# Four convolution layers on one core: the first layer's scratch rows laid out row by row, and 25 instead of 27 rounds of matmuls in its first block

## The chip, the cores and the metric

One core of a Trainium2 chip runs the whole program. The metric is the device time of one execution in microseconds (us), lower is better. Engines are named as the profile names them: PE is TensorE (PEld its weight loads), DVE is VectorE, ACT is ScalarE, POOL is GpSimd, SP is SyncE, which issues most of the DMAs. A name with a q behind it (SPq, ACTq) is an engine's queue as it issues DMAs.

## What is computed

The input x is (4, 16, 512, 512), float32. Four layers follow, each of the form x = x + conv(gn(x)), where gn is a group norm over pairs of channels. Only the first layer's two blocks are touched by the change:

```
def _conv_reflect(x, w, bias, dil, pad):
    xp = jnp.pad(x, ((0, 0), (0, 0), (pad, pad), (pad, pad)), mode='reflect')
    out = lax.conv_general_dilated(xp, w, window_strides=(1, 1), padding='VALID', rhs_dilation=(dil, dil), ...)
    return out + bias[None, :, None, None]

def _denoise_block(x, w1, b1, w2, b2, w3, b3, a, b, c):
    trip = _triplets(x)          # each channel with the one before and after it: (B*T, 3, H, W)
    o = a*_conv_reflect(xf, w1, b1, 1, 2) + b*_conv_reflect(xf, w2, b2, 2, 4) + c*_conv_reflect(xf, w3, b3, 4, 8)
    return jnp.tanh(o).reshape(B, T, H, W)

y = _denoise_block(gn(x), blk1 ...)
z = _denoise_block(y, blk2 ...)
x = x + z
```

So each block is a 5x5 convolution at dilations 1, 2 and 4 over three neighbouring channels, summed and put through tanh. The later layers are a 3x3 convolution on quantized values, a box filter of 17x17, and a complex convolution between two Fourier transforms.

## The kernel before

**Values as two halves.** A float32 value goes to TensorE as a high and a low float16. A row in the DRAM scratches `xs` (input of block 1) and `ys` (output of block 1, input of block 2) is `RW` = 1056 float16: the high row of 528 (512 and 8 mirrored columns at either side), then the low row of 528; 2112 bytes.

**Chunks, groups, units.** An image has 8 pairs of channels. A unit u is one half (256 rows) of one pair of output channels; block 1 is u = 0 to 63, block 2 is u = 64 to 127. A unit has four groups g, a group four chunks of 16 rows; the running number of a group is n = 4u + g. A chunk's window holds 32 rows (16 and 8 above and below) of four channels: 128 partitions. The windows of a unit's 16 chunks are the tile `c_w` (`win[half]`, 128 x 16 x 1056); two of them alternate. For p > 0 only the 64 partitions of the new channel pair are loaded, since the other pair is there from two units before.

**Products (line 734).** A matmul takes a weight matrix of 128 x 32 (32 = 16 rows x 2 channels) and 512 columns of one chunk's window, shifted by one of nine column offsets. Four of them, for the four chunks of a group, fill the 128 partitions of a PSUM bank: one round. There are nine column offsets and three products of halves for each (high x high, high x low, low x high): 27 rounds in block 1. Block 2 uses that offsets -2, -1, 1, 2 need only the middle 24 rows, so 96 partitions: its weight and row order puts those 24 rows into partitions 0 to 95, and copies bring low rows into the free 32. `near` (`c_n`, copied by VectorE, lines 669 and 670) holds the 96 partitions of high rows with 32 of low rows below them; `twice` (`c_2`, copied by ScalarE, lines 817 and 818) holds the remaining 64 low partitions once for each of two offsets. Eight rounds become four on `near` and two on `twice`: 25. The copies of group n + 1 are made at the start of the loop's turn for group n, on both engines.

**What follows a group.** ScalarE evicts with tanh (`evict`, line 812). In block 1 VectorE makes the high half (`halves`, line 639) and the low half (line 641) in `c_y`, POOL mirrors the pads (line 911), and SP stores two to three copies of each channel's rows to `ys` (`store_y`, line 974); in units where SP's queue is crowded POOL issues those stores (line 882). In block 2 VectorE adds x, and takes statistics and extremes (lines 649 to 658), and SP stores x1.

**The input's way into block 1.** The normalized input is made beside the products, one tile of 8 x 16 rows x 16 for a channel pair at a time (32 tiles): four steps, one in each of four groups that follow one another, a tile every seven groups. v0 takes statistics on VectorE (lines 465, 467), v1 (line 473) and v2 (lines 477 to 481) the spread, the root and the scaling, v3 the low half (line 487). In the group after v0 and after v1 TensorE sums over the partitions with two small fp32 matmuls, 15 rounds into the group (lines 711, 715). ScalarE makes the root and the high half (line 803). POOL mirrors pads (line 859), SP stores to `xs` (line 929). Group 15 also holds VectorE's `channel_weights` (lines 556 to 585) for later layers, group 22 `scaled_weights`, and from u = 60 on a table.

**Order on SP.** In each group SP loads the window part of unit u + 2 that TensorE has just left (line 956 in block 1: four chunks a group, two DMAs for each channel pair; line 952 in block 2: eight chunks every second group, four DMAs), then stores. Before the loop it loads units 0 and 1. In DRAM the scratches of the kernel before keep, for a channel pair, [row in chunk 16][channel 2][chunk 32][RW], so that the chunks of one partition follow one another: 4 x 2112 bytes are one piece in block 1, 8 x 2112 in block 2.

## Time and profile before

| | |
|---|---|
| median of three runs | 5166.97 us (5162.87 to 5169.14) |
| the profiled execution | 5166.33 us |
| its span | 5164.4 us |
| PE busy | 4871.3 us (94%) |
| DVE busy | 3723.3 us (72%) |
| ACT busy | 3384.5 us (66%) |
| POOL busy | 1510.5 us (29%) |
| mean granted clock of TensorE | 0.989 |
| DMA | 1167.24 MB, 226 GB/s |

How to read it: "busy" is the share of the span in which an engine had an instruction; matmuls are pipelined, so PE at 94% is not PE at its peak. A timeline row gives start, duration, engine and line, what it writes and reads, how many alike follow one another, and in brackets the idle time before it with what ended it. DMA share is the mean busy share of the 16 DMA engines, and may pass 1 where packets of one engine overlap. PEclk is the granted clock of TensorE, 1.00 for the 2.4 GHz level and 0.50 for the 1.2 GHz level.

### The profile page before, as it was taken

The page shows a single profiled execution, that of the slowest core. Times are in us where ns is not written, and L with a number is a line of the kernel's source. Part 1 is how long each engine was busy: PE and PEld are TensorE (multiplying, and loading weights), DVE is VectorE, ACT ScalarE, POOL GpSimd, SP SyncE. Part 2 cuts the span into 40 slices and gives each one's busy share as a digit, 9 for nine tenths or more (in the row PEclk, how much of TensorE's full clock was granted, in tenths as well). Part 3 has the DMA queues.
Part 4 walks back from the last instruction along what each step waited for, and adds up shares of the span by engine and source line. Part 5 has one row for each costly group of instructions (what it writes and reads, how often), then busy time and mean ns, then how long its engine had stood idle before and what let it go on. Part 6 is the DMA issues. An engine that isn't in the chain of part 4 may idle for free. (4 is left out here: it accounts for less than half of the span.)

```text
span 5164.4 us, 176760 instructions
## 1 busy us (share of the span) xinstructions
PE 4871.3 (94%) x76605; PEld 2923.4 (57%) x76605; DVE 3723.3 (72%) x6707; ACT 3384.5 (66%) x3511; POOL 1510.5 (29%) x1801
## 2 busy tenths in 40 slices
PE   4999999999999999999999979997777899999998
PEld 2444544444447967568875533444555566666665
DVE  4653553553534888888888868887999688888888
ACT  1222222231224888888888878885998798989897
POOL 1102102102102221222222100003776355555556
PEclk9999999999999999999999989999999999999999
DMA  8778778778757877878787769996886466666664
GB/s 259 232 247 267 234 247 267 238 246 258 236 191 204 242 222 229 237 223 238 233 226 241 223 221 325 323 324 238 308 309 261 111 151 152 150 154 149 154 149 119
DMA packets 368016, 1167.24 MB, mean 226 GB/s; under 512 B 75689, under 2 KB 76328, under 8 KB 297386
## 3 DMA queue, kind: packets, MB, share of 16 engines
q1 hardware_dynamic: 342040, 1131.78, 72.2%
q0 software_dynamic: 23040, 21.76, 1.5%
q8 instruction: 606, 9.93, 0.8%
q10 hardware_dynamic: 2162, 2.39, 0.2%
q14 instruction: 168, 1.38, 0.1%
HBM read 683.58 MB, written 453.51 MB: 220 GB/s over the span
## 5 line engine op out<-in xcount | busy, mean ns | idle before, releaser
L734 PE MATMUL c_p<-c_w,wc 128*32 128x512 f16 x27648 | 1518.7, 380 | 25.3 <-DMA c_w<-xs 19.9
L812 ACT ACTIVATE c_t<-c_p,cbias,cscale 128x512 f32<-128x512 f32 x512 | 397.9, 777 | 1273.7 <-PE c_p L734 1273.7
L734 PEld LDWEIGHTS c_p<-c_w,wc 128*32 128x32 f16 x27648 | 753.1, 96 | 762.3 <-issue 26.6
L734 PE MATMUL c_p<-c_w,w 128*32 128x512 f16 x19456 | 1145.0, 379 | 3.5 <-issue 3.4
L734 PEld LDWEIGHTS c_p<-c_w,w 128*32 128x32 f16 x19456 | 758.5, 96 | 316.3 <-issue 7.1
L639 DVE TENSOR_SCALAR c_y<-c_t 128x512 f16<-128x512 f32 x256 | 111.8, 437 | 644.7 <-ACT c_t L812 593.6
L1818 PE MATMUL f_P<-f_qh,f_wt 64*64 64x512 f16 x4608 | 545.7, 378 | 1.8 <-DVE f_t L1714 1.8
L1818 PE MATMUL f_P<-f_hl,f_wt 64*64 64x512 f16 x4608 | 545.3, 379 | 0.0
L817 ACT ACTIVATE c<-c_w 64x2052 f16<-64x2052 f16 x256 | 492.5, 1924 | 11.9 <-DMA c_w<-ys 5.7
L818 ACT ACTIVATE c<-c_w 64x2052 f16<-64x2052 f16 x256 | 492.9, 1925 | 6.2
L1979 POOL TENSOR_TENSOR f_y<-f_y,f_x 128x512 f32<-128x512 f32 x256 | 330.8, 1292 | 449.2 <-DVE f_hl L1693 443.1
L1578 POOL TENSOR_TENSOR e_hl<-e_g,e_hl 128x2048 f16<-128x2048 f32 x63 | 257.2, 4082 | 610.4 <-ACT e_hl L1528 610.4
L1714 DVE SCALAR_TENSOR_TENSOR f_t<-f_P,f_kk,f_ci 128x256 f32<-128x256 f32 x1024 | 423.5, 476 | 13.0 <-PE f_P L1818 7.9
L911 POOL COPY c_y<-c_y 128x16 f16<-128x16 f16 x512 | 87.6, 202 | 1129.6 <-DVE c_y L641 1129.6
L1779 PE MATMUL f_qp<-f_hil,f_gT 128*128 128x260 f16 (+1 forms) x3120 | 392.2, 275 | 4.0 <-DVE f_qh L1698 4.0
L1818 PEld LDWEIGHTS f_P<-f_hl,f_wt 64*64 64x64 f16 x4608 | 233.0, 106 | 255.0 <-issue 77.7
L1207 PE MATMUL d_pp<-d_q,wq 128*128 128x512 f16 x1536 | 346.4, 381 | 17.7 <-DVE d_q L1104 17.7
L1985 POOL TENSOR_TENSOR f_t<-f_t 128x512 f32<-128x512 f32 (+1 forms) x260 | 333.1, 1281 | 70.6 <-DVE f_hl L1693 70.6
L1953 ACT ACTIVATE f_y<-f_P,f_kk,sv 128x256 f32<-128x256 f32 x512 | 260.8, 560 | 128.1 <-PE f_P L1818 121.9
L649 DVE TENSOR_TENSOR a_x<-c_t,a_x 128x512 f32<-128x512 f32 x256 | 190.8, 745 | 193.6 <-ACT c_t L812 178.8
L1779 PEld LDWEIGHTS f_qp<-f_hil,f_gT 128*128 128x128 f16 (+1 forms) x3120 | 294.6, 98 | 41.8 <-issue 5.0
L734 PE MATMUL c_p<-c_n,w 128*32 128x512 f16 x4096 | 314.3, 379 | 0.0
(275 smaller groups left out, 7826.3 us busy)
## 6 DMA issues: line engine op xcount, KB each, us to landing
c_w<-xs SPq DMA_DIRECT2D x576, 264.0 KB, 8.2
d_x<-x SPq DMA_DIRECT2D x128, 1024.0 KB, 7.6
x<-d_x SPq DMA_DIRECT2D x128, 1024.0 KB, 5.1
c_w<-ys SPq DMA_DIRECT2D x144, 528.0 KB
xs<-a_hl SPq DMA_DIRECT2D x70, 1056.0 KB, 11.1
a_x<-in_x SPq DMA_DIRECT2D x256, 256.0 KB, 5.7
a_x<-in_x SPq DMA_DIRECT2D x128, 512.0 KB, 4.8
x<-a_x SPq DMA_DIRECT2D x512, 128.0 KB, 6.1
```

The source lines that it names most:

```text
L734: t = p.matmul(pg[32 * j:32 * j + 32, :], weights[:, var], source[:, j, at:at + NW], start=start, stop=stop, tile_position=(0, 32 * j))
L812: s.activation(tt_[n % 3][:, :], pp[:, n % 4, :], ACT.Tanh, bias=cbias[:, blk:blk + 1], scale=cscale[:, blk:blk + 1]).then_inc(c_act, 1)
L817: s.activation(twice[n % 2][64:128, :, PAD - 2:PAD - 1 + NW], w[0:64, :, PW + PAD + 1:PW + PAD + 2 + NW], ACT.Copy).then_inc(c_2b, 1)
L818: s.activation(twice[n % 2][0:64, :, PAD - 2:PAD - 1 + NW], w[0:64, :, PW + PAD - 2:PW + PAD - 1 + NW], ACT.Copy).then_inc(c_2a, 1)
L1207: t = p.matmul(pp[:, 4 * (i % 2) + j, :], wq[:, wl, dx, :], qt[i % NQ][:, j, dx:dx + NW], start=(i < 2 and dx == 0 and wl == 0), stop=(i > ...
L1578: q.tensor_tensor(h[:, 1], gt[i % 2][:, :, :], h[:, 0], ALU.subtract).then_inc(e_lo, 1)
L1714: v.scalar_tensor_tensor(dst[0:n, z], src[:, 256 * z:256 * z + 256], k_[0:n, off + z:off + z + 1], cc_[0:n, j, z], op, ALU.mult).then_inc( ...
L1779: t = p.matmul(qp[0:n, a_, 0:260], T[:, xl, 1 - a_, kx, 0:n], hil[:, wl, 1 - a_, kx, :], start=z == 0, stop=z == 5)
L1818: t = p.matmul(P[64 * z:64 * z + 64, bank, :].rearrange("p (a i) -> p a i", a=2), w[k0:k0 + 64, wl, f, :], r[k0:k0 + 64, l, :, 0:256], sta ...
L1953: s.activation(y0[i % 3][0:n, z], P[0:n, 0, 256 * z:256 * z + 256], ACT.Identity, bias=k_[0:n, 6 + z:7 + z], scale=inv(i)).then_inc(f_y0, 1)
L1979: q.tensor_tensor(y0[i % 3][:, :, :], y0[i % 3][:, :, :], par(xin[i % NXF][:, :]), ALU.add).then_inc(f_ax, 1)
L1985: q.tensor_tensor(t1[i % 3][0:n], t1[i % 3][0:n], t2[i % 2][0:n], ALU.add).then_inc(f_aw, 1)
```

## The change

In the first layer:

- `xs` and `ys` are laid out row by row: [row 512][channel 2][RW] for a pair of channels. `constants()` orders the selection matrix by the new places of rows.
- A store of y names 64 rows as one dimension instead of 4 x 16. A store of the input names rows of 2112 bytes instead of pieces of four.
- Both blocks load windows as block 2 did in time and size (eight chunks, after every second group), now as one part of 48 (row, channel) places and two of 8 for each channel pair, of 2112 bytes each; at an image's upper and lower end the parts leave out the rows that aren't there, and one more part of 40 is loaded.
- Both blocks make `near` and `twice` and run 25 rounds. In block 1 VectorE makes three of the copies and ScalarE one; in block 2 two and two, as before.
- In block 1 the high half of y moves from VectorE to ScalarE (`high`), with its wait for earlier stores.
- The weights of both blocks stand in one tile in the same row order (`wall`), so the 24 reordering DMAs of u = 8 to 19 and their semaphore go, POOL makes the near weights once at the start, for both blocks, and clears two chunks' windows at the image's ends, and the swapped copy of the weights is made with two DMAs of the whole tile.

The diff, cut:

```diff
-        self.xs = nc.dram_tensor("xs", (NB, NC // 2 + 1, 16, 2, 32, RW), F16).ap()
-        self.ys = nc.dram_tensor("ys", (NB, NC // 2 + 1, 16, 2, 32, RW), F16).ap()
+        self.xs = nc.dram_tensor("xs", (NB, NC // 2 + 1, NH, 2, RW), F16).ap()
+        self.ys = nc.dram_tensor("ys", (NB, NC // 2 + 1, NH, 2, RW), F16).ap()
...
             e.wait_ge(c_ld[u % 2][g // 2], 16 * (3 + at_edge(u % 2, g)) * n)
...
-                def halves(u, g):
+                def low(u, g):
...
-                    v.wait_ge(c_act, n + 1)
-                    if u >= 2 and g == 0:
-                        stored(v, u)
-                    elif g == 0:
-                        v.wait_ge(a_sd, n_xs(2))
-                    v.tensor_scalar(hi, tl[:, :], YS, None, ALU.mult).then_inc(c_hi, 1)
                     v.wait_ge(c_hi, n + 1)
                     v.scalar_tensor_tensor(lo, tl[:, :], YS, hi, ALU.mult, ALU.subtract).then_inc(c_lo, 1)
...
                     v.tensor_copy(near[n % 2][0:96], w[0:96, :, 0:PW]).then_inc(c_nh, 1)
                     v.tensor_copy(near[n % 2][96:128], w[64:96, :, PW:RW]).then_inc(c_nl, 1)
+                    if n < 4 * NU:
+                        v.tensor_copy(twice[n % 2][0:64], w[0:64, :, PW:RW]).then_inc(c_2a, 1)
...
                     for di in (2, 3, 5, 6):
-                        t = four(wu[:, 1, :, di], rows4, PAD + DX[di])
-                    if not blk:
-                        for di in (2, 3, 5, 6):
-                            for xl in range(2):
-                                t = four(wu[:, 0, :, di], rows4, xl * PW + PAD + DX[di], stop=(di, xl) == (6, 1))
-                    if blk:
...
+                        four(wu[:, blk, 1, :, di], rows4, PAD + DX[di])
+                    if n == 0:
+                        p.wait_ge(w_wn, 12)
+                    wnear = wn[pr % 2][:, blk]
+                    p.wait_ge(c_nh, n + 1)
+                    p.wait_ge(c_nl, n + 1)
+                    for e, di in enumerate((2, 3, 5, 6)):
+                        four(wnear[:, :, e], near[n % 2], PAD + DX[di])
+                    p.wait_ge(*((c_2c, n - 4 * NU + 1) if blk else (c_2a, n + 1)))
+                    p.wait_ge(c_2b, n + 1)
+                    four(wnear[:, :, 4], twice[n % 2], PAD - 2)
+                    t = four(wnear[:, :, 5], twice[n % 2], PAD - 1, stop=True)
...
+                def high(u, g):
+                    n = 4 * u + g
+                    s.wait_ge(c_act, n + 1)
+                    if u >= 2 and g == 0:
+                        stored(s, u)
+                    elif g == 0:
+                        s.wait_ge(a_sd, n_xs(2))
+                    s.activation(yt[u % 2][:, g, 0, PAD:PAD + NW], tt_[n % 3][:, :], ACT.Copy, scale=YS).then_inc(c_hi, 1)
...
-                        q.dma_start(dram(ys, pair(b, gp, slot, 16 * half) + g * 4 * RW, [[RW, 4], [VP, 16], [1, RW]]), y[m::2]).then_inc(c_yp[u % 2], 16)
+                        q.dma_start(dram(ys, pair(b, gp, 256 * half + 64 * g, slot), [[YP, 64], [1, RW]]), y[m::2]).then_inc(c_yp[u % 2], 16)
...
-                        e.dma_start(dram(xs, pair(b, gp, slot), [[VP, 16], [4 * RW, 8], [1, 4 * RW]]),
-                                    halves_of(i)[c][:, :, :, :].rearrange("p r l w -> p (r l w)")).then_inc(a_sd, 16)
+                        e.dma_start(dram(xs, pair(b, gp, 0, slot), [[YP, 16], [64 * YP, 8], [16 * YP, 4], [1, RW]]),
+                                    halves_of(i)[c][:, :, :, :].rearrange("p r l w -> p r (l w)")).then_inc(a_sd, 16)
...
+                    f, n = int(first), 8 - first - last
+                    parts = [(0, 48, -4, f, n), (96, 8, -8, f, 8 - f), (112, 8, 20, 0, 8 - last)]
+                    parts += [(16, 40, 0, 0, 1)] * first + [(0, 40, -4, 7, 1)] * last
                     for gp in (0, 1) if p == 0 else (p + 1,):
...
+                        for to, count, row, j, banks in parts:
+                            e.dma_start(win[half][to + gp % 2:to + 2 * count:2, 4 * g + j:4 * g + j + banks],
+                                        dram(src, pair(b, gp, 256 * half + 64 * g + 16 * j + row), [[RW, count], [16 * YP, banks], [1, RW]])).then_inc(c_ld[half][g // 2], 16)
...
-                        if u + 2 < NU and not late:
-                            load(u + 2, g)
-                        if NU <= u + 2 < 2 * NU and g % 2:
+                        if u + 2 < 2 * NU and not late and g % 2:
                             load(u + 2, g - 1)
```

## Rows read from the trace of the kernel before

**Rows 1.** The page's engine line, and line 734 by tiles: count, ns min/median/max, first and last start.
```profile
PE 4871.3 (94%) x76605; PEld 2923.4 (57%) x76605; DVE 3723.3 (72%) x6707; ACT 3384.5 (66%) x3511; POOL 1510.5 (29%) x1801
...
L734 PE MATMUL c_p<-c_w,wc x27648: 377/379/634, 70.9 to 1631.3; 128*32 128x512 f16 x199
...
L734 PE MATMUL c_p<-c,w x2048: 377/379/391, 1636.4 to 3023.4; 128*32 128x512 f16 x187
```

**Rows 2.** Timeline of ACT in block 1: start us, duration us, line, operands [idle before].
```profile
805.15 0.78 ACT L812 ACTIVATE c_t<-c_p,cbias,cscale 128x512 f32<-128x512 f32 x1 [6.17 <-PE c_p L734]
811.42 0.78 ACT L812 ACTIVATE c_t<-c_p,cbias,cscale 128x512 f32<-128x512 f32 x1 [5.49 <-PE c_p L734]
...
819.24 3.62 ACT L803 ACTIVATE a_hl<-a_x 128x4096 f16<-128x4096 f32 x1 [0.78 <-DVE a_x L481]
...
829.35 0.78 ACT L812 ACTIVATE c_t<-c_p,cbias,cscale 128x512 f32<-128x512 f32 x1 [5.06 <-PE c_p L734]
835.19 0.78 ACT L812 ACTIVATE c_t<-c_p,cbias,cscale 128x512 f32<-128x512 f32 x1 [5.06 <-PE c_p L734]
```

**Rows 3.** Timeline of ACT in block 2.
```profile
1902.24 0.78 ACT L812 ACTIVATE c_t<-c_p,cbias,cscale 128x512 f32<-128x512 f32 x1 [0.73 <-PE c_p L734]
1903.04 1.92 ACT L817 ACTIVATE c<-c_w 64x2052 f16<-64x2052 f16 x1
...
1907.64 0.78 ACT L812 ACTIVATE c_t<-c_p,cbias,cscale 128x512 f32<-128x512 f32 x1 [0.73 <-PE c_p L734]
```

**Rows 4.** Timeline of PE: the longest waits in block 1.
```profile
128.63 5.34 PE L734 MATMUL c_p<-c_w,wc 128*32 128x512 f16 x60 [7.63 <-DMA c_w<-xs]
...
198.54 0.59 PE L794 MATMUL a_p<-c2b,ones 128*128 128x1 f32 x2 [4.78 <-DVE c2b L585]
...
502.28 3.18 PE L734 MATMUL c_p<-c_w,wc 128*32 128x512 f16 x28 [3.64 <-DMA c_w<-xs]
...
1273.20 10.63 PE L734 MATMUL c_p<-c_w,wc 128*32 128x512 f16 x168 [5.26 <-DMA c_w<-xs]
```

**Rows 5.** Busy time by stretch: engines, PEclk, DMA share, GB/s; after such a wait.
```profile
502.00:506.00 4.00, 3.72 (x36) 1.40 (x40) 3.78 (x7) 0.00 (x0) 2.65 (x6) 0.50 1.01 344
```

**Rows 6.** Timeline of DVE in block 2: the copies into near.
```profile
1905.56 0.70 DVE L669 COPY c_n<-c_w 96x2112 f16<-96x2112 f16 x1
1906.29 0.70 DVE L670 COPY c_n<-c_w 32x2112 f16<-32x2112 f16 x1
```

**Rows 7.** Timeline of DVE in block 1, over the steps of one input tile.
```profile
800.09 4.84 DVE L465 BATCH_NORM_STATS2 a_st<-a_x 128x6 f32<-128x512 f32 x8
804.96 0.37 DVE L467 BATCH_NORM_AGGREGATE a_mv<-a_st 128x2 f32<-128x48 f32 x1
806.03 0.43 DVE L639 TENSOR_SCALAR c_y<-c_t 128x512 f16<-128x512 f32 x1 [0.70 <-ACT c_t L812]
806.49 0.69 DVE L641 SCALAR_TENSOR_TENSOR c_y<-c_t,c_y 128x512 f16<-128x512 f32 x1
...
822.89 4.47 DVE L487 TENSOR_TENSOR a_hl<-a_x,a_hl 128x4096 f16<-128x4096 f32 x1 [2.50 <-ACT a_hl L803]
```

**Rows 8.** Timeline of DVE: the start of the channel weights; first and last of the scaled ones.
```profile
179.16 0.60 DVE L556 COPY rp<-a_p 128x432 f32<-128x432 f32 x1
...
230.82 0.15 DVE L245 TENSOR_SCALAR c2b<-a_p 128x1 f32<-128x1 f32 x1
...
240.57 0.15 DVE L541 TENSOR_SCALAR sv<-sv 128x1 f32<-128x1 f32 x1
```

**Rows 9.** Busy time by stretch, columns as in rows 5: three short stretches by their DMAs.
```profile
1542.00:1545.00 3.00, 3.00 (x64) 1.63 (x56) 0.15 (x1) 0.78 (x1) 0.17 (x1) 1.00 0.24 86
1871.00:1873.00 2.00, 2.00 (x44) 1.19 (x39) 1.97 (x4) 1.98 (x2) 0.00 (x0) 1.00 1.19 270
883.00:886.00 3.00, 3.00 (x64) 1.49 (x60) 0.80 (x2) 0.00 (x0) 2.70 (x6) 1.00 1.04 304
```

**Rows 10.** DMA queue over 1542 to 1545 us: packets, MB, share of 16 engines.
```profile
q1 hardware_dynamic: 129, 0.26, 23.6%
```

More of the change, by code:

```diff
@@ L17 @@
 RW = 2 * PW
-CP = 32 * RW
-VP = 2 * CP
+YP = 2 * RW
 DX = [-8, -4, -2, -1, 0, 1, 2, 4, 8]
@@ L40, in slot @@
     def slot(row, chan):
-        h8, s = ((1, 0), (0, 0), (1, 1), (0, 1))[row // 8 + 1]
-        v8 = row + 8 * h8 - 16 * s
-        return 8 * (2 * v8 + chan % 2) + 4 * s + 2 * h8 + chan // 2
+        place = row + (32, 4, 4, 4, 4, 4, 4, 8)[row // 4 + 2]
+        return 4 * place + 2 * (chan % 2) + chan // 2
     sel = np.zeros((27, 3, 32, 128), np.float32)
@@ L397, in stored, with at_edge @@
                     e.wait_ge(done[u % 2], n)
-        def n_win(u, g):
-            return sum((1 + (place(r)[2] == 0)) * (64 * (g % 2 == 0) if place(r)[0] else 32) for r in range(u % 2, u + 1, 2))
+        def at_edge(half, g):
+            return (half, g // 2) in ((0, 0), (1, 1))
         def rows_in(e, u, g):
-            if place(u)[0]:
-                g = g // 2 * 2
-            e.wait_ge(c_ld[u % 2][g], n_win(u, g))
-        def doubled(n):
-            return 4 * NU <= n < 8 * NU
-        def n_copied(n):
-            return n - 4 * NU + 1
+            n = sum(1 + (place(r)[2] == 0) for r in range(u % 2, u + 1, 2))
+            e.wait_ge(c_ld[u % 2][g // 2], 16 * (3 + at_edge(u % 2, g)) * n)
         def four_rows(e, n):
@@ L420, in four_rows @@
             rows_in(e, u, g)
[L421 removed]
+            if n >= 2:
+                e.wait_ge(c_pe, n - 1)
             return win[u % 2][:, 4 * g:4 * g + 4]
[L424 to L429 removed]
         def table_of(u):
@@ L684, in _ @@
                 v0(2), v1(2)
+                copies(0)
                 for u in range(2 * NU):
@@ L700, in _ @@
                             table(table_of(u), g // 2)
-                        (total if blk else halves)(u, g)
+                        (total if blk else low)(u, g)
                         if blk:
@@ L838, in _ @@
                 s.wait_ge(a_v, mark["wc"])
+                copies(0)
                 for u in range(2 * NU):
@@ L848, in _ @@
                         evict(u, g)
+                        if u < NU:
+                            high(u, g)
                         if st_ == 2:
```

95 lines of the change are left out of this document (33 added, 62 removed).

## The prediction

> **What bounds the kernel now.** I read the page first, then single lines: TensorE is busy 94% of the span, and the matmuls of the first layer alone run from 70.9 us to 3023.4 us of 5164.4, block 1 until 1631.3 and block 2 after it [rows 1]. Nothing outside these two blocks is changed, so the question is what ends one group of four chunks in each. The ACT timeline gives the period, since one eviction (line 812) closes each group: 835.19 - 829.35 = 5.84 us in block 1 [rows 2], 1907.64 - 1902.24 = 5.40 us in block 2 [rows 3]. Block 1 has 27 rounds of four matmuls in a group and block 2 has 25; 5.84 / 27 and 5.40 / 25 are both 0.216 us. So both blocks run at the pace of TensorE. Two groups of each input tile last 6.26 us (811.42 - 805.15 = 6.27 [rows 2]): the two small fp32 matmuls of the statistics cost 0.42 us each. Beside that there are single stalls on loaded windows and on VectorE's chain for the later layers [rows 4], and a stall of some length is paid twice: from 502 to 506 us the granted clock is 0.50 [rows 5], the 1.2 GHz level, after the wait of 3.64 us.
>
> **The sum is made against 5166.3 us**, the profiled execution's own time (span 5164.4 and 1.9 around it); the median of the runs is 5167.0, so the two stand for each other.
>
> **Two rounds fewer in block 1.** 27 rounds become 25 in 256 groups: 0.216 x 2 = 0.432 us each. The first eight groups give nothing: group 8 waits 7.63 us for its window [rows 4] at 128.6, a chain of tile 2 (split, mirrored pads, store, load) through SP that starts no earlier than now, so a faster TensorE only waits longer. I count 248 x 0.432 = -107 us. The window of group 8 now comes in one piece of eight chunks instead of four, which I put at +1.5 us (bounds -3 and +4, about one load more).
>
> **Copies that both blocks now need.** In block 2 this work is there already: VectorE's two copies 0.70 us each [rows 6], ScalarE's 1.92 us each [rows 3]. Block 1 adds to VectorE three copies and takes away the high half (0.43 us [rows 7]): with the spacing of 0.73 from start to start, +2.2 - 0.46. ScalarE gets one copy of 1.92 and the high half: 4096 elements cost 3.62 us [rows 2], so 512 cost about 0.45 plus a fixed part of some 0.2, an estimate of 0.64. Mean load of VectorE: 2.2 + 0.6 + (5.24 + 0.8 + 4.4 + 4.4) / 7 = 4.9 of 5.4 us; ScalarE: 1.9 + 0.8 + 0.6 + (3.6 + 2.8) / 7 = 4.2. Neither is the bound on average, but the order within a group matters, for VectorE takes its work in program order.
> Group k ends at 0. Eviction 0.78, high half 0.64, low half 0.61 and the hand-overs: low(k) is done at 2.2. Copies for the next group but one 2.2: 4.4. If a tile's first step lies here, eight statistics and their sum take 5.24 (800.09 to 805.33 [rows 7]): 9.7. TensorE wants that result 15 rounds into the group after: 5.40 + 15 x 0.216 = 8.65. It waits **1.0 us**, where before it did not (2.0 + 5.2 = 7.2 against 5.84 + 3.24 = 9.1). The following steps fit: after the low half of the input (4.4 us, line 487 [rows 7]) the near copies come 1.7 us before their group asks for them. 28 tiles: +28 us, bounds 0 (if copies run beside statistics better than I add them) and 50 (a wait of 1.8, with POOL's pads in the way of the copies). A wait of 1 us is short of the 3.64 that cost clock.
> **VectorE's long chains.** The channel weights hold VectorE from 179.16 until TensorE gets c2b at 198.54 [rows 8, 4], 19.4 us. Before, TensorE waited 4.78 us for them, and lost some 3.4 us more to the slower clock (as after 502 us: 28 matmuls in 3.18 us where 1.5 are due [rows 4]). Now the copies of group 17 are queued behind that chain: low(14) ends 5.5 us after its group (a tile's last step lies before it), copies 2.2, chain 19.4, low half and first copies 2.1, together 29.2; group 17 asks at 2 x 5.4 + 19 x 0.216 + 0.9 = 15.8. Wait 13.4, with clock 16.8, against 8.2: +8.7. The scaled weights (230.82 to 240.72 [rows 8]) cost nothing before; now the copies of group 24 lie behind them, wait about 5.6 and 3.4 of clock: +9.
>
> **Stores over 64 rows.** Each store of y names 64 rows of 2112 bytes; before, its DRAM side has an outer dimension of 4. From 1542 to 1545 us, with these stores alone in flight, the DMA share is 0.24, so 3.8 of 16 engines work, and a packet takes 0.236 x 48 / 129 = 0.09 us [rows 9, 10]. In one u (four groups) these four engines carry 144 of them, 13.4 us; loads 18 packets of 8448 bytes at 4 x 0.110 (304 GB/s over 16 engines, 883 to 886 us [rows 9]) 7.9; the input's stores 4.0 and the input's loads 3.5 at the same price: 28.8 us against the 24.4 that a u took. So these prices are a fifth too high, and those four engines were full; this is why windows came late at the image boundary (3.64 and 5.26 us [rows 4], with clock 6.6 each).
> The Trainium skill (DMA: Bandwidth & Descriptors, Why a DMA increments its semaphore by 16 and not by 1) says that the engines used are the largest number up to 16 that divides the outermost dimension of both sides; by that rule, the trace agrees: 4 gives 3.8.
> After: 36 packets on every engine, 3.3 us.
> **Input tiles of 48, 8 and 8 rows, packets of 2112 bytes.** A window half takes 64 x 8 packets: three on each engine for each of eight chunks from the 48 rows, and if the 8 rows go to eight engines, 16 more there. At 0.110 and, for the 8 rows, at the price of block 2's loads (1871 to 1873 us: 270 GB/s at a share of 1.19, 0.148 us for 2112 bytes of a packet's own time [rows 9]) that is 2.6 + 2.4 = 5.0 us, 11.3 in a u (2.25 halves). Input store 4.0, input load 3.5, y 3.3: 22.1 us on the fullest engines; divided by the same 1.18, 18.7, against TensorE's 4 x 5.40 + 0.9 = 22.5. So DMA stays under TensorE, with some 17% to spare, and costs nothing while that holds. The two boundary stalls and a smaller third (about 16 us) mostly go: -12. In block 2 the fullest engines go from 5 x 1.19 to 5.0 us for a half: -3, or nothing.
> The Trainium skill (SBUF — State Buffer, Door 1: The DMA port swizzle) speaks against this tile shape: sixteen neighbouring partitions reach only 4 of 16 ports, about 109 GB/s, so that each 8-row part (135 KB) would take an estimated 1.24 us however many engines work on it. The sum by it would be 155 instead of 148 ns for these packets, 0.3 us in a u. No row shows the parts alone.
> **Small things.** The row-major layout keeps the bytes. SP issues 7 loads in a u instead of 9. The wait for y's stores goes from VectorE to ScalarE; it was rare. Weights for both blocks are now made once at the start by POOL (twelve short copies), hidden behind the statistics; the swap of partitions waits for them, ahead of u = 2, which alone needs it.
> **Sum:** 5166.3 - 107 + 1.5 + 28 + 8.7 + 9 - 12 - 3 = **5092 us** (5091.5).
>
> **Rivals.**
> (a) TensorE never waits in block 1: copies and statistics overlap enough. 5092 - 28 = 5064 us. For: block 2's VectorE does 5 us of work in 5.4 without a stall. Against: the order above.
> (b) The DMA engines become the bound of block 1. If the fullest need 23.1 to 23.9 us in a u, block 1 lasts 64 x 23.1 = 1478 to 1530, plus 19 for the start, against 1560: 5103 to 5155, and most likely about 5125. For: 22.1 at full price is close to 22.5, and the bytes of block 1 pass in 1450 us instead of 1560. Against: the same prices overstate today's load by a fifth.
> (c) Slower than before, the same place with a price that decides: all load packets at the dearest rate and more. It decides from 24.1 us in a u (64 x 24.1 + 19 = 1561), and that is what comes out if all 90 load packets, not the 36 of the 8-row parts alone, cost 0.148: 13.3 + 10.8. With 10% more for each, a cost of short packets that no row shows, it is 25.4, block 1 lasts 1645 and the whole 5251 us.
> (d) The change doesn't do what it says: y's stores stay on few engines. 13.4 + 11.3 + 7.5 = 32 us in a u, 27 with the factor, +170 us. Against: the outer dimension is 64 on both sides.
>
> **How the numbers follow.** Forecast 0.55 (own range 5072 to 5112), (a) 0.13, (b) 0.24, (c) and (d) 0.08. The range leaves out the top of (b), (c), (d) and the bottom of (a): 5056 to 5150. Less than 0.2% (10 us), which a measurement of this kernel can't tell from no change, is 5157 to 5177: the ends of (b) and (c) that meet there. Faster 0.85, same 0.08, slower 0.07.
>
> **What would show it.** Eviction spacing in block 1 of 5.40; matmuls on c_n and c from the start; PE waiting about 1.0 us for line 467's result once a tile; waits of 13 and 6 us near groups 17 and 24; no DMA share of 0.24 with y's stores in flight; no wait for a window near 500 and 1270 us. Wrong if TensorE waits for windows in steady state (b, c), or if near copies come late in each tile (VectorE over its bound).

## The result, and the profile after

The changed kernel takes 5135.65 us (median of five, 5130.48 to 5147.41) against 5166.97 us before: a ratio of 0.9947, 95% interval 0.9929 to 0.9964. The sign of the forecast held; of the forecast gain of 75 us less than half came (31.3). The time lies outside the forecast's own range (5072 to 5112 us) and inside its wider one (5056 to 5150), where the prediction had placed rival (b). The page's engine line after (busy us, share of the span, instructions), and its line of the DMA queue that SP feeds (packets, MB, share of 16 engines), beside [rows 1]:

```profile
PE 4773.7 (93%) x74557; PEld 2754.2 (54%) x74557; DVE 4136.3 (81%) x7219; ACT 4039.4 (79%) x4023; POOL 1627.4 (32%) x1803
q1 hardware_dynamic: 486200, 1126.77, 75.7%
```

TensorE is busy for 97.6 us less than before, more than the time fell by: it waits more. What it waits for in block 1, by the view of waits from 80 to 1610 us (engine, tile, line; released by; us in total, times, longest):

```profile
PE c_p L710 <- DMA c_w<-xs: 52.1, 10, 13.0
PE a_p L690 <- DVE a_mv L449: 24.3, 26, 3.5
PE c_p L710 <- DVE c_n L646: 18.4, 2, 13.0
PE c_p L710 <- issue: 5.1, 11, 0.9
```

The second and the third line are waits that the prediction named, in its sizes. The first is not: 52.1 us for windows, of which the prediction had left group 8's (7.63 and 1.5) and the first window's, 3.4 before and 13.0 now. Where they lie, from PE's timeline (start, duration, operands, count [idle before, releaser]), beside [rows 4]:

```profile
80.49 5.93 PE L710 MATMUL c_p<-c_w,wc 128*32 128x512 f16 x76 [13.03 <-DMA c_w<-xs]
...
147.33 5.76 PE L710 MATMUL c_p<-c_w,wc 128*32 128x512 f16 x60 [11.91 <-DMA c_w<-xs]
220.36 1.90 PE L710 MATMUL c_p<-c_n,wc 128*32 128x512 f16 x16 [12.97 <-DVE c_n L646]
266.89 1.90 PE L710 MATMUL c_p<-c_n,wc 128*32 128x512 f16 x16 [5.43 <-DVE c_n L646]
504.22 4.29 PE L710 MATMUL c_p<-c_w,wc 128*32 128x512 f16 x76 [1.16 <-DMA c_w<-xs]
520.96 5.85 PE L710 MATMUL c_p<-c_w,wc 128*32 128x512 f16 x76 [5.19 <-DMA c_w<-xs]
```

The first two are the first window and group 8's; the last two are the second image's start, the kind of place where windows were late before too. The waits of 13.03, 12.97, 11.91, 5.43 and 5.19 us are followed by slow matmuls (76 of them in 5.93 or 5.85 us instead of 4.29, 16 in 1.90 instead of 1.04); the one of 1.16 is not.

**Where the time went, by stretches.** One eviction closes a group, so the times between evictions in ACT's timeline divide both blocks without gaps. "Start" is everything until group 8's eviction (n = 8); "boundaries" are n = 57 to 68, 122 to 136 and 186 to 200, around the three changes of image; "clear" is the rest of block 1 from n = 26 on. The column "forecast" takes the prediction's terms to the same stretches (with 0.432 us for each group, the first ones too; so its sum is 3 us more than the prediction's).

| stretch | before | after | difference | forecast |
|---|---|---|---|---|
| start, to n = 8 | 137.1 | 155.7 | +18.6 | -1.9 |
| n = 8 to 16 | 50.9 | 46.7 | -4.2 | -3.4 |
| n = 16 to 26, VectorE's long chains | 67.6 | 79.5 | +11.9 | +13.4 |
| clear, 190 groups | 1133.3 | 1073.2 | -60.1 | -54.1 |
| three boundaries, 39 groups | 242.8 | 249.2 | +6.4 | -28.9 |
| block 2 (n = 255 to 511) | 1392.1 | 1385.5 | -6.6 | -3 |
| last eviction | 3023.8 | 2989.9 | -33.9 | -77.9 |

The miss of 44 us stands in two rows: 20.5 at the start, 35.3 at the boundaries, and 12 given back by the others. Both are places where TensorE waits for windows. So the question for the runs was what makes a window late there, and whether the parts that came as forecast came for the forecast reason.

### The profile page after: what moved, and what is told of

Same layout as the page of the kernel before. It is cut to its first block and busy times, and to the rows that moved or that the text cites. A ratio compares the mean times of both kernels' runs of the same rounds, so it can differ in the third digit from the quotient of the medians.

```text
span 5128.7 us, 174422 instructions
## 1 busy us (share of the span) xinstructions
PE 4773.7 (93%) x74557; PEld 2754.2 (54%) x74557; DVE 4136.3 (81%) x7219; ACT 4039.4 (79%) x4023; POOL 1627.4 (32%) x1803
## 5 line engine op out<-in xcount | busy, mean ns | idle before, releaser
L710 PE MATMUL c_p<-c_w,wc 128*32 128x512 f16 x38912 | 2271.3, 380 | 56.7 <-DMA c_w<-xs 52.1
L710 PEld LDWEIGHTS c_p<-c_w,wc 128*32 128x32 f16 x38912 | 1202.4, 96 | 979.0 <-DMA c_w<-xs 44.3
L800 ACT ACTIVATE c<-c_w 64x2052 f16<-64x2052 f16 x512 | 984.7, 1923 | 95.9 <-DMA c_w<-xs 83.7
L710 PE MATMUL c_p<-c_n,wc 128*32 128x512 f16 x8192 | 587.7, 380 | 19.1 <-DVE c_n L646 18.4
L899 POOL COPY c_y<-c_y 128x16 f16<-128x16 f16 x512 | 191.1, 401 | 973.2 <-DVE c_y L617 973.2
L802 ACT ACTIVATE c<-c_w 64x2052 f16<-64x2052 f16 x256 | 492.9, 1925 | 6.3
L645 DVE COPY c_n<-c_w 96x2112 f16<-96x2112 f16 x512 | 389.2, 760 | 61.3 <-DMA c_w<-xs 61.3
L1693 DVE SCALAR_TENSOR_TENSOR f_t<-f_P,f_kk,f_ci 128x256 f32<-128x256 f32 x1024 | 423.6, 476 | 12.7 <-PE f_P L1797 7.4
L617 DVE SCALAR_TENSOR_TENSOR c_y<-c_t,c_y 128x512 f16<-128x512 f32 x256 | 177.2, 692 | 269.3 <-ACT c_y L796 267.3
L710 PEld LDWEIGHTS c_p<-c_n,wc 128*32 128x32 f16 x8192 | 268.6, 96 | 217.5 <-DVE c_n L645 19.3
L646 DVE COPY c_n<-c_w 32x2112 f16<-32x2112 f16 x512 | 368.3, 719 | 15.9
L710 PE MATMUL c_p<-c,wc 128*32 128x512 f16 x4096 | 365.1, 380 | 0.9 <-issue 0.9
```

Of the source, the lines that this page charges most:

```text
L645: v.tensor_copy(near[n % 2][0:96], w[0:96, :, 0:PW]).then_inc(c_nh, 1)
L646: v.tensor_copy(near[n % 2][96:128], w[64:96, :, PW:RW]).then_inc(c_nl, 1)
L710: t = p.matmul(pg[32 * j:32 * j + 32, :], weights[:, var], source[:, j, at:at + NW], start=start, stop=stop, tile_position=(0, 32 * j))
L800: s.activation(twice[n % 2][64:128, :, PAD - 2:PAD - 1 + NW], w[0:64, :, PW + PAD + 1:PW + PAD + 2 + NW], ACT.Copy).then_inc(c_2b, 1)
L802: s.activation(twice[n % 2][0:64, :, PAD - 2:PAD - 1 + NW], w[0:64, :, PW + PAD - 2:PW + PAD - 1 + NW], ACT.Copy).then_inc(c_2c, 1)
L1693: v.scalar_tensor_tensor(dst[0:n, z], src[:, 256 * z:256 * z + 256], k_[0:n, off + z:off + z + 1], cc_[0:n, j, z], op, ALU.mult).then_inc( ...
```

## The experiments

The times below are medians, the ratios are to the kernel before on the same chip, whose median there was 5162.0 us (runs 1 to 4), 5174.9 (5 to 7), 5166.7 (8 to 10) and 5165.8 (11 and 12). Differences between runs of different groups carry these few us with them. Where a rate of the loads is given, it is that of a stretch near 75 us, before the loop, in which only window loads are in flight.

**1. The two parts of 8 rows as one of 16.** The rows in places 48 to 63 are not the right ones; bytes and packets are kept but for 8 places more in the chunk at an image's end.

```diff
-parts = [(0, 48, -4, f, n), (96, 8, -8, f, 8 - f), (112, 8, 20, 0, 8 - last)]
+parts = [(0, 48, -4, f, n), (96, 16, 0, 0, 8)]
```

> Edit: the two 8-row parts of each window load become one part of 16 (row, channel) places, the same bytes and the same number of 2112 byte packets, so the outer rows of every window hold other rows than they should (this part of the computation is changed). Theory A, the parts of 8 places are what makes the loads slow, since they keep to eight engines: the loads alone (66 to 80 us, 207 GB/s in the changed kernel, 281 before) come back to about 280 GB/s, the first matmul of line 710 starts at 76 instead of 80.5, the waits for windows of block 1 (52 us) fall under 20, and the time is about 5105 us. Theory B, packets of 2112 bytes instead of 8448 are slow by themselves: 207 GB/s stays, and the time stays at 5136 within 5. Theory C, sixteen neighbouring partitions are too few: the rate rises only a little, to 230 GB/s, 5125 us.

Measured: 5140.5 us, ratio 0.9951 (0.9935 to 0.9966), as the change itself. But not the same inside: start 145.8 (-9.9), boundaries 227.4 (-21.8), and the clear stretch 1098.6 (+25.4). The waits from 80 to 1610 us:

```profile
PE c_p L710 <- issue: 37.8, 38, 1.9
PE c_p L710 <- DVE c_n L646: 18.6, 2, 13.1
PE a_p L690 <- DVE a_mv L449: 17.5, 20, 1.9
PE c_p L710 <- DMA c_w<-xs: 12.3, 1, 12.3
```

The late windows at the boundaries are gone, though the rate rose hardly (219 GB/s from 74 to 80 us, 206 in the changed kernel). I read this as the work of how evenly the 16 engines are loaded, though no row shows the engines singly. In their place came waits for "issue", that is, for nothing that the profile names. A look at one, PE's timeline:

```profile
643.89 2.11 PE L710 MATMUL c_p<-c_w,wc 128*32 128x512 f16 x36
647.76 1.48 PE L710 MATMUL c_p<-c_w,wc 128*32 128x512 f16 x24 [1.76 <-issue]
```

The DMA records of the instruction queue (q8) have a packet of 16 KB that lands at 646.14 us, 1.6 before the matmuls go on; the ones that land at 637.24 and 654.83 stand 1.5 and 1.7 before the ends of two more such waits. Of the 45 gaps of over 1.2 us from one matmul's start to the next between 300 and 2950 us, 29 have an instruction packet that lands 1.2 to 1.8 us before their end (44 of 56 in run 12 below). Of all moments 8 to 9% have one, and of the 28 such gaps in the changed kernel 3, so no more than chance. I read this as TensorE's own program arriving late behind the data. No run takes the fetches away, so it stays a reading.

**2. The kernel before with its load as four pieces of a row.** Meant to show what shorter packets cost by themselves.

```diff
-    win[half][gp % 2 + 2 * h8:128:4, 4 * g:4 * g + 4].rearrange("p k w -> p (k w)"), ... [[CP, 16], [RW, 2], [1, 4 * RW]]
+    win[half][gp % 2 + 2 * h8:128:4, 4 * g:4 * g + 4], ... [[CP, 16], [RW, 2], [RW, 4], [1, RW]]
```

> Edit: the kernel before, only block 1's window loads walk four pieces of 2112 bytes instead of one of 8448; partitions, engines, order and bytes are the same. Theory B (short packets are slow by themselves): the loads alone from 66 to 80 us fall from 281 to about 210 GB/s, windows come late at the start and at the image boundaries, 5190 us or more. Theory A: 270 to 280 GB/s stay, 5167 us within 8.

Measured: 5163.67 us, ratio 1.0004 (0.9991 to 1.0017). The packets in the trace stayed at 8448 bytes: pieces that follow one another on both sides are one piece, however they are written. The run says nothing on short packets; it shows how far the stretches of one kernel differ between two profiles (boundaries 235.9 and 242.8, start 138.4 and 137.1).

**3. The change with 27 rounds and without copies in block 1**, so layout, loads and the moved high half alone.

```diff
+if not blk:
+    for di in (2, 3, 5, 6):
+        for xl in range(2):
+            t = four(wu[:, 0, 0, :, di], rows4, xl * PW + PAD + DX[di], stop=(di, xl) == (6, 1))
+    t.then_inc(c_pe, 1)
+    return
```

> Edit: the changed kernel, but block 1 runs its 27 rounds straight from the windows and makes no copies; layout, loads, stores and the move of the high half stay. If DMA bounds the start and the image boundaries and TensorE the rest, evictions stand 5.84 us apart in steady state, the first matmul starts late as in the changed kernel (80 us against 70.9), and the boundaries wait less than in the changed kernel, since TensorE asks later; sum: 5167 + 9 + about 10 for group 8, less some boundary time, 5175 us (5165 to 5190). Rival: the loads cost nothing and VectorE's copies made the whole shortfall: 5160 or less, as the stores' better spread would then show alone.

Measured: 5176.54 us, ratio 1.0028 (1.0012 to 1.0043): the layout alone costs some 14 us. The start is the changed kernel's (154.9 us), so the loss there has nothing to do with the copies. The boundaries take 234.6 us, 5.2 over what 39 groups need without any wait (229.4, 5.88 us a group with the small matmuls of two tiles); with 25 rounds they take 249.2, 36.7 over it (212.5). Fewer rounds made the boundaries no shorter but longer: TensorE comes earlier to a window that comes no earlier (it waits 23.8 us for windows there, and 2.4 in this run).

**4. The first step of a tile ahead of the copies in VectorE's order.**

```diff
+if s == 0:
+    v0(i)
 if 4 * u + g + 1 < 8 * NU:
     copies(4 * u + g + 1)
-if i is not None:
+if i is not None and s:
```

> Edit: the changed kernel, but VectorE takes a tile's statistics (v0) ahead of the copies of the next group, in the same turn of the loop. My step says that TensorE's wait of 0.9 us for them in each of 27 tiles (24.3 us in all) is on the path: it goes, and the time is 5136 - 24 = 5112 us. Rival: in block 1 the DMAs are the bound on average, so what is won here is given back as longer waits for windows: 5130 or more, with the waits for c_w risen from 52 us.

Measured: 5116.77 us, ratio 0.9906 (0.9882 to 0.9929), 19 us less than the change. TensorE's waits for the statistics between 80 and 1610 us fell from 24.3 us (26 times) to 2.3 (once). The copies are early enough even after 5 us of statistics, so the tile term came from the order of the two. The waits for issue rose from 5.1 to 14.2 us, so not all that was won shows in the time.

**5. Windows as one part of 64 places.** The rows stand in another order than the weights expect. Bytes and packets are kept but for the chunk at an image's end, of which 64 places are loaded instead of 48; the DMAs of a channel pair fall from three to one.

```diff
-parts = [(0, 48, -4, f, n), (96, 8, -8, f, 8 - f), (112, 8, 20, 0, 8 - last)]
-parts += [(16, 40, 0, 0, 1)] * first + [(0, 40, -4, 7, 1)] * last
+parts = [(0, 64, -8, f, n)]
+parts += [(0, 64, 0, 0, 1)] * first + [(0, 64, -16, 7, 1)] * last
```

> Edit: each window load of the changed kernel (48 + 8 + 8 places) becomes one part of 64 places over all 128 partitions, again the same bytes in packets of 2112 bytes, so windows hold rows in other places than they should (this part of the computation is changed). The 16-place form of the run before gave 234 GB/s for the loads alone where 207 and 281 stand for the changed kernel and the kernel before. Theory: the uneven spread over engines and partitions is all of it; one part of 64 is even, gives 270 to 285 GB/s at 66 to 80 us, the first matmul at 75 us or earlier, boundaries without waits, 5105 to 5115 us. Rival: short packets are the rest; 234 GB/s stays, and the first matmul at 77 us as in the 16-place form. Beside that, if TensorE's short waits without a releaser (38 us in the 16-place form, 5 in the changed kernel) come from loads on the upper engines, they stay here, some 20 to 40 us, and the time is 5130.

Measured: 5070.22 us, ratio 0.9803 (0.9775 to 0.9831), 65 us less than the change. The same two stretches of before, of the change and of this run (stretch, length, busy us and counts of PE, PEld, DVE, ACT, POOL, PEclk, DMA share, GB/s), first before:

```profile
74.00:80.00 6.00, 6.00 (x112) 2.98 (x104) 0.40 (x1) 1.27 (x2) 0.00 (x0) 1.00 1.02 276
300.00:1500.00 1200.00, 1188.10 (x21598) 583.11 (x21593) 558.74 (x936) 313.19 (x298) 165.64 (x568) 1.00 0.79 247
```

the changed kernel:

```profile
74.00:80.00 6.00, 0.00 (x0) 0.00 (x0) 0.00 (x0) 0.00 (x0) 0.00 (x0) 1.00 1.07 206
300.00:1500.00 1200.00, 1153.12 (x20768) 608.73 (x20760) 906.90 (x1380) 848.77 (x721) 253.15 (x575) 0.99 0.92 252
```

and one part of 64:

```profile
74.00:80.00 6.00, 6.00 (x94) 2.87 (x88) 5.29 (x15) 4.55 (x4) 0.00 (x0) 1.00 1.05 401
300.00:1500.00 1200.00, 1177.57 (x21434) 605.16 (x21430) 922.79 (x1407) 869.72 (x740) 269.09 (x597) 1.00 0.81 257
```

In all three the engines are fully busy in the short stretch, at 276, 206 and 401 GB/s. A packet of 2112 bytes takes 86 ns here (median, 74 to 80 us) and 156 in the changed kernel; before, 8448 bytes take 491. So short packets were never the trouble: sent in this form, they beat the long ones of before. Of the 62 us until the last eviction, 27.1 come from the start (128.6 us) and 33.6 from the boundaries (215.6), next to nothing from elsewhere. The prediction's boundaries, 242.8 - 28.9 = 213.9 us, are what this form gives.

**6. VectorE's long chains in pieces.** `channel_weights` in five pieces (n = 15, 16, 22, 23, 29), `scaled_weights` in three (36, 37, 43), their users later, and the order of run 4.

```diff
-if (u, g) == (3, 3):
-    channel_weights()
-if (u, g) == (5, 2):
-    scaled_weights()
+if 4 * u + g in (15, 16, 22, 23, 29):
+    next(chains[0])
+if 4 * u + g in (36, 37, 43):
+    next(chains[1])
```

> Edit: statistics first as in the fourth run, and VectorE's channel weights are cut into five pieces (groups 15, 16, 22, 23, 29) and the scaled weights into three (36, 37, 43), with TensorE's and ScalarE's small parts moved behind them. My step says that the waits of 13 and 5.4 us near groups 17 and 24, with the clock lost behind them (3.4 us each), come from these two chains in front of the copies: both go, -20 to -25 us against the fourth run's 5117: 5095. Rival: the DMAs are behind anyway at that time and the wait moves to the windows: 5110 or more.

Measured: 5101.45 us, ratio 0.9864 (0.9839 to 0.9888), the best whole computation of this study. The waits from 80 to 1610 us:

```profile
PE c_p L723 <- DMA c_w<-xs: 49.9, 9, 13.3
PE c_p L723 <- issue: 18.2, 22, 1.8
PE a_p L703 <- DVE a_mv L449: 5.2, 3, 2.7
PE c_p L723 <- DVE c_n L656: 0.9, 4, 0.3
```

The copies' wait went from 18.4 to 0.9 us, and n = 16 to 26 from 79.5 to 61.9 (80.7 in run 4): 17.6 to 18.8 us, wait and slow clock together. The windows' wait stands where it was; the waits for issue rose, from 5.1 us in the changed kernel and 14.2 in run 4 to 18.2.

**7. The same, and tile 2's store and the window loads of u = 2 earlier on SP.** The first part of tile 4's load also goes one group later. The edit, cut:

```diff
                 for u in range(2):
                     for g in (0, 2):
                         load(u, g)
+                store_xs(2)
                 load_x(3)
```

> Edit: the sixth run's kernel, and on SP the store of input tile 2 goes ahead of the load of tile 3 and of the swapped weights, and the first part of tile 4's load goes behind the loads of unit 2. Theory: group 8 (147 us against 129 before) is late because SP, held up by the slow window loads, issues that store at 117 us instead of 97; issued at about 101, it lands by 115 and group 8 starts at 130 to 135: 12 us less than the sixth run, some 5083. Rival: the order doesn't matter, since the same bytes have to pass before group 8: group 8 at 145, same time as the sixth run.

Measured: 5103.19 us, ratio 0.9863 (0.9839 to 0.9887): nothing more. The first window loads of u = 2 are issued at 121.80 us instead of 139.72 and group 8 waits only 2.46 us, but tile 3's input is now loaded later, and TensorE waits for its statistics instead (17.5 us for a_mv from 80 us on, once 12.40, where run 6 has 5.2). The start is 151.0 instead of 158.4 us; later stretches give 4 of the 7 back.

**8. Parts of 56 and 8.** The computation is whole: rows -4 to 23 stand in places 0 to 55, rows -8 to -5 behind them. On top of run 6.

```diff
-place = row + (32, 4, 4, 4, 4, 4, 4, 8)[row // 4 + 2]
+place = row + (36, 4, 4, 4, 4, 4, 4, 4)[row // 4 + 2]
-parts = [(0, 48, -4, f, n), (96, 8, -8, f, 8 - f), (112, 8, 20, 0, 8 - last)]
+parts = [(0, 56, -4, f, n), (112, 8, -8, f, 8 - f)]
```

> The split chains of the run before (5101.5), and the window's rows in another order: -4 to 23 in places 0 to 55 and -8 to -5 in places 56 to 63, so that a channel pair takes one part of 56 places and one of 8 instead of 48, 8 and 8. The computation is whole. Theory E (each engine's share of the places decides): the fullest engines carry 56/14 + 8/8 = 5 of 64 places, as with 48/16 + 8/8 + 8/8 = 5, so the loads alone stay at some 210 GB/s (the changed kernel's 207 between 66 and 80 us) and the time at 5101, within 5. Theory P (a part that lands in few partitions is slow, and a quarter of the bytes came in such parts, now an eighth): the rate between 66 and 80 us halfway from 207 to the 371 of one part of 64, some 280 GB/s; the waits of TensorE for c_w fall from 49.9 us to 20 to 25, and the time to 5075 (5065 to 5085). A third of the DMAs fewer also shortens SP's issue before the loop.

Measured: 5128.78 us, ratio 0.9926 (0.991 to 0.9942), 27 us slower than run 6. Block 1 stayed as theory E has it (start 156.1, boundaries 243.3). The rate is even lower, 187 GB/s at a share of 0.94 where the other forms reach 1.02 to 1.08. That is 14/16 of 1.07, as if 14 of the 16 engines worked. Block 2 got 20 us longer (1406.9), with 9.9 us of waits for issue from 1700 to 2900 us instead of 1.1. Theory P fell: a smaller clustered part didn't raise the rate.

**9. Four parts of 16**, each into 32 neighbouring partitions, on the changed kernel. Rows at the image's ends are not the right ones.

```diff
+parts = [(32 * q, 16, 8 * q - 8, 0, 8) for q in range(4)]
```

> The changed kernel with a channel pair's window loaded as four parts of 16 places, each into 32 neighbouring partitions; the rows at the image's ends are not the right ones, so the output differs; bytes and packets are those of one part of 64. All parts divide evenly over 16 engines. Theory E (only the engines' shares count): as with one part of 64, 371 GB/s between 66 and 80 us, no waits for c_w over some 10 us, 5070 us plus a few for the fourfold DMAs. Theory P (few partitions at a time): as slow as the part of 16 beside 48 or slower, under 234 GB/s, waits for c_w above 22 us, time 5130 or more.

Measured: 5152.34 us, ratio 0.9968 (0.9956 to 0.998), loads alone at 220 GB/s (78 to 84 us). Theory E as I had put it fell as well: evenly loaded engines don't give 401. But even parts went again with what run 1 had shown: boundaries 226.0, and late windows only at the start, two of them, 22.3 us in all.

**10. One part of 64, and the chains in pieces** (runs 5 and 6 together; rows in another order, as in 5).

> The split chains (5101.5) with the load as one part of 64 places; which rows stand in the windows differs from the reference's, so the output differs. It shows what is left once both causes are taken away. If the two are separate: 5101.5 - 65 (what the one part of 64 gave to the changed kernel: 5135.6 to 5070.2) = 5036, less what both had removed (the wait for v0's statistics isn't shared by them): 5030 to 5045. If the split chains' gain is partly given back where loads no longer hide it: 5045 to 5060.

Measured: 5038.13 us, ratio 0.9755 (0.9736 to 0.9773). The two gains add: 5135.65 - 65.4 - 34.2 = 5036.1. It is a floor for this design, not a kernel: its windows hold the wrong rows.

**11. Two parts by chunks**: each with all 64 places and four chunks, on the changed kernel. **12. Two parts of 32 places**, each into 64 neighbouring partitions. Rows at the image's ends are not the right ones in both.

```diff
+parts = [(0, 64, -8, j, 4) for j in (0, 4)]              # run 11
+parts = [(64 * q, 32, 16 * q - 8, 0, 8) for q in range(2)]   # run 12
```

> The changed kernel with a channel pair's window loaded in two parts by chunks: 64 places (all 128 partitions with the other pair) and four chunks each. The rows at the image's ends are not the right ones, so the output differs. One part of 64 places gave 403 GB/s between 72 and 78 us and 5070 us; parts of 48 and 16, of 48, 8 and 8, of 56 and 8, and four of 16 gave 224, 215, 188 and 177 to 220. Theory N (each further DMA of a channel pair costs rate): two parts as one of 48 and one of 16, 220 to 240 GB/s, and 5130 to 5140 us. Theory S (what decides is that a part's places divide over the 16 engines so that each engine writes to its own eighth partitions): as one part of 64, 390 to 410 GB/s, 5070 to 5080 us.

> The changed kernel with a channel pair's window loaded as two parts of 32 places, each into 64 neighbouring partitions; the rows at the image's ends are not the right ones, so the output differs. 32 places divide evenly over 16 engines, two each. Theory N (the number of DMAs): the same rate as by chunks. Theory S: worse than by chunks; if the rate follows the partitions that a part reaches, between the 220 GB/s of four parts of 16 and the 403 of one part of 64, some 290 to 330 GB/s between 72 and 78 us, and 5080 to 5110 us.

Measured: 5067.13 us (ratio 0.9815, 0.9799 to 0.9832) and 5203.06 us (1.0072, 1.0053 to 1.0092). Same bytes, same packets, same number of DMAs, 136 us apart. The two stretches of run 11:

```profile
74.00:80.00 6.00, 6.00 (x72) 2.69 (x76) 5.29 (x15) 5.14 (x4) 0.00 (x0) 1.00 1.05 408
300.00:1500.00 1200.00, 1178.49 (x21469) 613.23 (x21465) 924.20 (x1409) 871.59 (x741) 269.76 (x597) 1.00 0.81 258
```

and of run 12, with its waits from 80 to 1610 us:

```profile
74.00:80.00 6.00, 2.50 (x24) 1.09 (x28) 2.49 (x4) 2.55 (x2) 0.00 (x0) 1.00 1.07 220
300.00:1500.00 1200.00, 1119.76 (x19840) 575.52 (x19835) 877.67 (x1338) 814.76 (x690) 244.19 (x550) 0.99 0.96 244
```

```profile
PE c_p L710 <- issue: 68.8, 68, 3.4
PE a_p L690 <- DVE a_mv L449: 18.7, 21, 2.5
PE c_p L710 <- DVE c_n L646: 17.6, 2, 12.2
PE c_p L710 <- DMA c_w<-xs: 13.2, 1, 13.2
```

Two DMAs that each cover all 64 places run at 408 GB/s, two that each cover one half of the partitions at 220. So not the number of DMAs decides (theory N) but the places that one DMA covers. Reach alone isn't all of it: each of the two parts of 32 in the kernel before goes to every fourth of the 128 partitions, in packets of 8448 bytes, and they ran at 276 GB/s. No run sends 32 places so spread in packets of 2112, so what part of that is the spread and what part the packet stays open. A half of the partitions is no faster than the quarter of run 9, against what I expected of it (290 to 330).

The Trainium skill (SBUF — State Buffer, Door 1: The DMA port swizzle) says that partitions 0 to 63 reach the same 8 of 16 ports as 0 to 31, some 218 GB/s, and 64 to 127 the other 8. The trace agrees: 220 for both forms, and nearly twice that with all 128. By the section "Can I just issue two DMAs to hit both halves?" of the same page of the Trainium skill two transfers are not fused, and all ports take part only within a transfer over all partitions; runs 11 and 12 agree.

## Why the prediction was right or wrong

The loads of these kernels side by side ("alone" is the rate of the short stretch; "share" the DMA share, and "issue" TensorE's waits for issue in us, both from 300 to 1500 us; the rest as in the table above):

| kernel | parts of a channel pair | alone | share | issue | start | boundaries | clear |
|---|---|---|---|---|---|---|---|
| before | 32 + 32 places, spread | 276 | 0.79 | 2.9 | 137.1 | 242.8 | 1133.3 |
| after | 48, 8, 8 | 206 | 0.92 | 3.9 | 155.7 | 249.2 | 1073.2 |
| run 8 | 56, 8 | 187 | 0.89 | 11.3 | 156.1 | 243.3 | 1064.7 |
| run 1 | 48, 16 | 219 | 0.93 | 34.4 | 145.8 | 227.4 | 1098.6 |
| run 9 | 16, 16, 16, 16 | 220 | 0.97 | 25.2 | 154.9 | 226.0 | 1091.9 |
| run 12 | 32, 32 by partitions | 220 | 0.96 | 64.4 | 148.2 | 233.2 | 1141.4 |
| run 11 | 64, 64 by chunks | 408 | 0.81 | 1.4 | 130.3 | 215.6 | 1069.3 |
| run 5 | 64 | 401 | 0.81 | 3.0 | 128.6 | 215.6 | 1071.1 |

**Two rounds fewer: right.** Evictions in undisturbed groups stand 5.41 us apart, as forecast (728.00 - 722.59 below), and in the 190 clear groups the rounds and the tile waits together gave 60.1 us, forecast 54.1. ACT's timeline over a tile's first steps, beside [rows 2]:

```profile
722.59 0.78 ACT L786 ACTIVATE c_t<-c_p,cbias,cscale 128x512 f32<-128x512 f32 x1 [2.02 <-PE c_p L710]
723.40 0.63 ACT L796 ACTIVATE c_y<-c_t 128x512 f16<-128x512 f32 x1
728.00 0.78 ACT L786 ACTIVATE c_t<-c_p,cbias,cscale 128x512 f32<-128x512 f32 x1 [2.02 <-PE c_p L710]
...
734.79 0.78 ACT L786 ACTIVATE c_t<-c_p,cbias,cscale 128x512 f32<-128x512 f32 x1 [3.41 <-PE c_p L710]
```

The high half takes 0.63 us (estimate 0.64).

**The tile term: right, place, size and cause.** Forecast 1.0 us a tile, 28 tiles. Measured 24.3 us in 26 waits. One of them, 3.55 us at 131 us, isn't of this kind, since run 3 has it too (3.1) without any copies; the other 25 are 20.7 us, 0.83 each. The one that belongs to the eviction of 734.79:

```profile
732.08 0.38 PE L690 MATMUL a_p<-a_mv,ones 128*128 128x1 f32 x2 [0.89 <-DVE a_mv L449]
```

No clock was lost (granted 1.00 from 732 to 736 us). Run 4 showed the cause by reordering two calls.

**VectorE's chains: right.** Forecast waits of 13.4 and 5.6 us for the copies queued behind them; measured 12.97 and 5.43, the net +11.9 for +13.4. Run 6 removed them, and the stretch from n = 16 to 26 became 17.6 us shorter. The program order of an engine is a queue as well: these chains of small instructions had cost TensorE 4.78 us and nothing before, and cost it 18.4 us as soon as something urgent was put behind them.

**The failed steps.** The prediction said of the windows: "DMA stays under TensorE, with some 17% to spare, and costs nothing while that holds. The two boundary stalls and a smaller third (about 16 us) mostly go: -12", and of the start +1.5, "about one load more". Both took the window load by an average: packets times a price, against a u of 22.5 us. The average did hold (the clear groups kept TensorE's pace), and so rival (b), a bound in steady state, did not happen either, though its 5125 lay closer to the measured time than the forecast. What decides at the start and at a boundary is how long one load takes when TensorE stands before it:

- The start: forecast -1.9, measured +18.6 us. The first matmul on a window starts at 80.49 us instead of 70.9 [rows 1], since twice the bytes must land (2.16 MB for eight chunks of two channel pairs, 1.08 for four) and at 206 instead of 276 GB/s: 10.5 us instead of 3.9. This came to 6.8 us at group 8: TensorE stood before it at 135.4 us, where it had begun it at 128.63 before. The rest, 11.91 us, is the wait for group 8's window, a chain through SP that ends at 147.33: SP needs 34.75 us to issue its 28 window loads where 32 took 20.73 before, and tile 2's store stands behind them. With the loads at 401 GB/s the start is 128.6, below what was forecast. SP's timeline after (start, duration, queue, line, count):

```profile
64.97 34.75 SPq L941 DMA_DIRECT2D c_w<-xs  x28
99.76 13.61 SPq L910 DMA_DIRECT2D a_x<-in_x  x8
113.42 3.22 SPq L995 DMA_DIRECT2D wc<-wc  x2
116.69 2.19 SPq L917 DMA_DIRECT2D xs<-a_hl  x2
```

- The boundaries: forecast -28.9, measured +6.4. The prediction put the old stalls down to four engines full with y's stores. Spreading these, with the new loads, did give 8 us with 27 rounds (run 3, 234.6 after 242.8, though run 2 shows that two profiles of one kernel differ by 7 there). But the loads brought, as I read it, an unevenness of their own: a boundary's window has two channel pairs, and the prediction sent each part of 8 to eight engines (no row shows the engines singly). Even parts at some 220 GB/s took the boundaries from 249.2 to 227.4, 226.0 and 233.2 (runs 1, 9, 12), without a late window there, and the full rate to 215.6 (runs 5, 11). What the full rate is worth is shown; that evenness is the cause of the first step is argued, since the waits for issue also slowed TensorE in those runs, and it came later to each window.

The prediction had both halves in hand. It counted 16 packets more on the fullest engines; and it quoted a rule of the ports against this tile shape, but priced it only for the two parts of 8 (0.3 us in a u), taking the 48 rows as free of it. Measured, the whole load runs at half the rate of 64 places in one DMA. No run loads the 48 places alone. If the parts pass one after the other, runs 9 and 1 give an estimate for them: a part of 16 runs at 220 GB/s, 48 and 16 together at 219, so the 48 run at about 219 too. At that rate a packet of the 48 takes 0.154 us of an engine, where the prediction had 0.110.

In the terms of the sum: +1.5 us for group 8's window was +18.7 (147.33 against 128.63), and -12 for the stalls at the boundaries was +23.3 (249.2 against 242.8 less 16.9 for the rounds). These two are the terms that failed.

**Stores over 64 rows: right.** Taken us by us from 300 to 1600 us, 95 of the 1300 stretches of 1 us had a DMA share of 0.22 to 0.28 before (four engines of 16, as [rows 9]); after, 7 have, and 5 in run 3. **Block 2**: -6.6 us for -3.

**Slips of the prediction that change nothing here.** Rival (d) by the way of (b) and (c) is 64 x 27 + 19 - 1560 = +187 us, not +170. A packet of y's stores at 0.088 us makes 12.7 us of 144, not 13.4. And SP's window loads in a u fell on average from 9 to 7.9, not to 7: the parts of 40 at the image's ends count too.

**What stays open.** Why 56 and 8 places are no faster than 48, 8 and 8, although 56 places cover nearly all partitions; which packets of a part of 48 hold one another up; why boundaries with fewer rounds took not just as long as with 27 but 15 us longer (249.2 and 234.6), of which the slow clock after waits is a part; and whether the waits for issue are the instruction packets held up behind data. For the last, the share from 300 to 1500 us goes some way (0.93 to 0.97 with 25 to 64 us, 0.81 with 1 to 3), but the changed kernel has 0.92 with 3.9, run 4 has 0.92 with 12.6 and run 6 has 0.93 with 17.4, so the share alone doesn't tell. A form that is both right in its rows and covers 64 places with each DMA was not found: the middle 24 rows must stand in the first 96 partitions, and the eight outer rows lie on both sides of them.

## What to carry to other kernels

Price a transfer twice: its bytes over the average, which tells whether an engine keeps its pace, and its own time from issue to landing at the rate of its shape, which tells what each start and each boundary costs when somebody stands before it. If a load must be cut, try to cut it by time or by chunks, so that each DMA covers all 64 places, before cutting it by groups of partitions: with the same bytes and count it was 408 against 220 GB/s here, and 136 us of the whole. And where work is added to an engine that runs in program order, look for the longest thing that will stand before it; putting the urgent part first, and the long chain in pieces, gave 34 us here (runs 4 and 6).

## What the runs showed of the hardware

- In the short stretch, packets of 2112 bytes take 86 ns each, with little spread (5% to 95%: 86 to 95), in DMAs over 64 places (runs 5, 11), and 151 to 169 ns (medians) in every other form tried, while the DMA share is 0.94 to 1.08 in all of them. A share near 1 is no sign that the rate can't be higher: it stood at 1.07 with 206 GB/s and at 1.05 with 401.
- Pieces that are neighbours on both sides go as one packet of 8448 bytes; rewriting the pattern in four pieces changed nothing (run 2).
- When the loads are slow in that way, TensorE stops for 1 to 3 us at a time without a semaphore, in all 68.8 us from 80 to 1610 us in run 12; in runs 1 and 12, 29 of 45 and 44 of 56 gaps above 1.2 us end 1.2 to 1.8 us after a 16 KB instruction packet lands.
- The granted clock was 0.50 from 148 to 152 us, after the wait of 11.91, and 1.00 from 732 to 736, around a tile wait of 0.89 us:

```profile
148.00:152.00 4.00, 4.00 (x40) 1.46 (x36) 3.07 (x8) 3.92 (x4) 0.43 (x1) 0.50 1.09 177
732.00:736.00 4.00, 3.92 (x70) 2.14 (x74) 3.21 (x8) 1.17 (x2) 0.75 (x2) 1.00 1.07 261
```
